# A graph network on one core: how often POOL waits for the landing of its own gathers and scatters

## The reference

```
h = maximum(layernorm(x), 0);  x = x + L0(h)   # three gcn hops and a product
h = maximum(layernorm(x), 0);  x = x + L1(h)   # mean over the edges, two layers with batch norm
h = maximum(layernorm(x), 0);  x = x + L2(h)   # six steps x = x + relu(agg/deg @ W.T + b)
h = maximum(layernorm(x), 0);  x = x + L3(h)   # two gcn hops with tanh between
```

## Time and profile before

| | us |
|---|---|
| median of 3 runs | 3292.27 (3290.51 to 3295.48) |
| the profiled execution | 3287.36 |
| its span | 3285.6 |
| POOL busy | 1442.2 (44%) |
| VectorE busy | 2032.4 (62%) |
| TensorE busy | 2527.2 (77%) |
| edge steps and hop 0, about | 19 to 749 |

### The profile page before, as it was taken

How to read it: one execution, slowest core, us unless ns; L and a number is a source line. 1 busy time by engine, 2 the same in 40 slices (tenths; PEclk the granted TensorE clock), 3 DMA queues, 4 the chain that set the end, 5 groups by cost and what they waited for, 6 DMA issues and landing times. The chain is left out here.

```text
span 3285.6 us, 46019 instructions
## 1 busy us (share of the span) xinstructions
PE 2527.2 (77%) x11251; PEld 1564.2 (48%) x11251; DVE 2032.4 (62%) x7784; ACT 1972.3 (60%) x4381; POOL 1442.2 (44%) x1507
## 2 busy tenths in 40 slices
PE   5767755558777678899999945799999999876840
PEld 2444434435555456445455422365655656543520
DVE  6544555558889766233333356687887878776630
ACT  1666755557777766455555558877777776764400
POOL 5555454545645264000000000176766767554576
PEclk8888877789888898899999966899999999987875
DMA  4655533445566565333333458866656656433311
GB/s 94 173 158 154 170 109 111 121 119 163 165 179 195 173 193 168 108 137 134 137 134 134 137 183 268 282 186 185 192 177 189 186 175 191 146 116 112 96 57 41
DMA packets 528965, 504.91 MB, mean 154 GB/s; under 512 B 58706, under 2 KB 389955, under 8 KB 528616
## 3 DMA queue, kind: packets, MB, share of 16 engines
q1 hardware_dynamic: 477388, 415.73, 39.2%
q0 software_dynamic: 47184, 85.73, 10.5%
q10 hardware_dynamic: 4172, 0.99, 0.2%
HBM read 246.45 MB, written 260.27 MB: 154 GB/s over the span
## 5 line engine op out<-in xcount | busy, mean ns | idle before, releaser
L1854 POOL DMA_INDIRECT h_G<-step_tab,row_i x294 | 287.1, 977 | 350.1 <-DMA step_tab<-l_NR 192.9
L1854 POOL DMA_INDIRECT h_M<-step_tab,row_i x294 | 284.3, 967 | 119.3 <-issue 86.3
L1567 DVE TENSOR_SCALAR b_Y<-b_BP,col 128x512 f32<-128x512 f32 x148 | 109.9, 742 | 354.5 <-PE b_BP L1521 354.5
L804 PE MATMUL a_PA<-a_H,w 128*128 128x512 f32 x504 | 263.2, 650 | 70.2 <-ACT a_H L968 63.4
L1549 ACT ACTIVATE b_Z<-b_BQ,bn 128x512 f32<-128x512 f32 x148 | 115.0, 777 | 256.7 <-PE b_BQ L1513 256.4
L1521 PE MATMUL b_BP<-b_Z,w 128*128 128x512 f32 x592 | 266.3, 592 | 0.0
L1609 POOL TENSOR_TENSOR b_d<-b_d,neghalf 128x1 f32<-128x1 f32 x1 | 0.6, 565 | 592.4 <-DVE b_d L1600 592.4
L2221 DVE TENSOR_TENSOR_SCAN h_T<-keep,h_T,h_P 128x512 f32<-128x512 bf16 x196 | 222.9, 1137 | 11.3 <-PE h_P L1972 2.1
L270 POOL DMA_INDIRECT h_G<-msg_tab,row_i x147 | 143.8, 978 | 195.5 <-issue 132.1
L239 ACT ACTIVATE a_NR<-a_XR,a_ln_nm,a_ln_rs 128x128 f32<-128x128 f32 x392 | 155.9, 485 | 106.3 <-DVE a_ln_nm L222 106.3
L239 ACT ACTIVATE a_HI<-a_X,a_ln_nm,a_ln_rs 128x128 f32<-128x128 f32 x490 | 201.0, 484 | 23.2 <-DVE a_ln_nm L222 23.2
(11 more groups left out here) (385 smaller groups left out, 6503.9 us busy)
## 6 DMA issues: line engine op xcount, KB each, us to landing
b_HI<-hin_tab SPq DMA_DIRECT2D x148, 256.0 KB, 2.8
y_tab<-b_Y SPq DMA_DIRECT2D x148, 256.0 KB, 2.0
l_Y<-y_tab SPq DMA_DIRECT2D x148, 256.0 KB, 4.0
l_X<-x_tab SPq DMA_DIRECT2D x148, 256.0 KB, 4.6
x_tab<-a_X SPq DMA_DIRECT2D x112, 256.0 KB, 4.3
hin_tab<-a_HI SPq DMA_DIRECT2D x112, 256.0 KB, 3.1
a_XR<-in_x SPq DMA_DIRECT2D x97, 256.0 KB, 4.5
out_rows<-l_O SPq DMA_DIRECT2D x97, 256.0 KB, 3.1
```

What stands on the lines that cost most here:

```text
L804: nc.tensor.matmul(PA[b][:, 0:nt * P], w[:, :], h[b][:, 0:nt, :].rearrange("p t d -> p (t d)"), start=True, stop=True).then_inc(done, 1)
L1567: nc.vector.tensor_scalar(Y[b][:, :], BP[b][:, :], col[:, C_B12:C_B12 + 1], None, ALU.add).then_inc(b_y, 1)
L1854: pool.indirect_dma_start(out=GR_[i % 2][b][:, k, :], out_offset=None, in_=table[:, :], in_offset=bass.IndirectOffsetOnAxis(ap=row_i[:, t ...
```

## The change

Four waits in POOL's program are dropped or thinned. In the E steps the wait for earlier scatters comes before every eighth scatter in place of every fourth. In `raw` the second half no longer waits until the first has landed. In hop 0 the last three slot reads no longer wait for the first four, and `raw(i + 1)` no longer waits for the slot reads. The waits for `x1`, for `sn.normed`, `xd_st`, `wd_set` and the one for `raw(i)` before the slot reads stay, and no transfer is added, dropped or moved.

```
                     for t in itertools.islice(scatters, NT if i == IT - 1 else 8):
-                        after(pool, slots_set, 16 * (t - t % 4))
+                        if t % 8 == 0:
+                            after(pool, slots_set, 16 * t)
                         pool.indirect_dma_start(out=node_tab[:, :], ...
...
                     after(pool, sn.normed, 2 * (i - 2) + b + 1)
                     after(pool, xd_st[i % 2][b], 16 * (i // 2))
-                    if b == 1:
-                        pool.wait_ge(xd_got[i % 2][0], 16 * SUB[0] * (i // 2 + 1))
                     for j in range(nt):
...
                 pool.wait_ge(xd_got[i % 2][1], 16 * SUB[1] * (i // 2 + 1))
                 for t in range(first_tile(i, 0), first_tile(i + 1, 0)):
-                    if t == first_tile(i, 1):
-                        pool.wait_ge(slot_got[i % 4], 16 * (sum(SUB) * (i // 4) + SUB[0]))
                     pool.indirect_dma_start(out=src_v[:, t, :], ...
-                pool.wait_ge(slot_got[i % 4], 16 * sum(SUB) * (i // 4 + 1))
                 if i + 1 < IT:
                     raw(i + 1)
```

## The result

The changed kernel takes 3177.33 us, the median of 4 runs (3170.21 to 3190.24), against 3291.4 for the kernel before (3290.51 to 3295.48, 4 runs): a ratio of 0.9654, 95% interval 0.9638 to 0.967. The forecast was 3185 with a range of 3173 to 3226. The profiled execution took 3173.83 us with a span of 3172.1, so its gain over the 3287.36 of before is 113.5 us, where the sum had 107.4. That holds for the chip it was timed on. On another, on which both kernels take longer, the changed one takes 1.0% more than the one before, which the last group of experiments is about.

A forecast was written before the change was run, and what follows sets the result against it. VectorE's 127.2 us of waits for POOL's gathers were taken as the bound up to 731 us. Edge steps and hop 0 steps of 20.9 us gave 107.4 us, so 3292.27 became 3185 us, range 3173 to 3226.

The forecast's parts named there:

- the sum: Whole kernel: edge-step and hop 0 savings put the last slot reads at 613.7 us instead of 721.06, a gain of 107.4 us.
- The edge steps: Before hop 0: 8.4 us from an earlier x1 and eight removed waits, 23.9 us, bring the first XD gather to 330.3 us.
- The landing of the last gathers in hop 0: POOL's wait before the slot reads in hop 0: taken as 3.76 us from the edge steps, between 2.2 and 5.2.
- the first rival: Edge steps and hop 0: landings grow with the burst, to 6.5 and 5.2 us; gain only 62.6 us, 3230 us; 14%.
- an estimate of 2.15 us: Landing of a 64 KB gather by the skill's rule; POOL's period falls under VectorE's 19.85 us, a gain of 115 us.
- The larger period rules, POOL's 20.9: Hop 0: POOL's period of 8.7 + 8.4 + 3.76 us sets the step, one microsecond over VectorE's.
- My second loop: Hop 0: VectorE's own step without its waits for XD, 19.85 us, with the 3.50 us wait for ScalarE's root kept.
- carried undiminished: After hop 0: later stages follow in a row with nothing of the change, so the 107.4 us gain reaches the end whole.
- a last third that takes a different time: Sign against the sum: the last third of the kernel takes a different time than before; no size given.
- the issues did not stretch: Rival on POOL's issues: packed against VectorE, a gather takes 1082 ns instead of 945; gain 67 us, 3225 us; 2%.
- the last rival: VectorE's chain shortens too: part of 74.6 us on products goes, with POOL's landing at its lower end; gain 125, 3167 us; 4%.
- The rival "slower": Hop 0: up to 15 transfers in flight delay each other; a landing of 11.5 us costs 27 us, 3319 us; 3%.

The follow-up runs named there:

- the last group of experiments: The unaltered changed kernel and three variants of it, on a chip where the kernel before takes 3620.19 us: unaltered 3664.94 us, variants 3739.19, 3680.78 and 3726.7 us.
- the runs meant to test it: Changed kernel with POOL held back once (3666.63 us), without landing waits (3755.2), with ScalarE's root earlier (3667.57), with both latter edits (3730.88); kernel before 3625.56 us there.

## Why the prediction was right

**The edge steps were 7.6 us better than worked out** (322.73 for 330.3). The gathers of step 5 start at 126.80, not 130.2, and were the ones bound by `x1`, as said (8.40 us of waiting). From there to the first `XD` gather it is 195.9 us, against 224.0 before, 28.1 less where the sum had 23.9. In the kernel before, POOL's waits of that stretch (138 to 363 us) are:

```profile
POOL node_tab L720 <- DMA a_XR<-in_x,src_i: 39.3, 9, 6.5
POOL node_tab L720 <- DMA node_tab<-own_v,end_i: 24.6, 8, 3.6
```

The eight removed waits were 24.6 us. The sum took them whole, though 0.3 us between two issues stays for each, so they give 22.2. The nine landing waits went from 39.3 to 33.9 us, 3.77 each, which gives another 5.4 that the sum did not have.

**The landing of the last gathers in hop 0 was the term mis-sized.** I took 3.76 us from the edge steps, between 2.2 and 5.2; it is 2.27. With it POOL's period is 8.7 + 8.4 + 2.3 = 19.4, and 19.47 is measured. The slot reads of step 13 start at 587.16 where the sum had 613.7; of these 26.5 us 7.6 come from the edge steps, 0.8 from the first landing and 13 x 1.39 = 18.1 from this. The prediction did name SP's traffic as what makes a landing long. Its mistake was to carry over the mean of the edge steps all the same, which mixes landings of 2.4 us, with SP quiet, and of 3.1 to 6.5, and not to ask where the last of seven gathers would fall: in the changed kernel that is behind SP's transfers. For the same reason the waits of four gathers were nearly twice those of three, which the first rival took as a sign of growth with the burst: those of three all stood where SP moved next to nothing (but for one at a share of 0.32). The rule of the Trainium skill in "DMA: Bandwidth & Descriptors", section "Anatomy of one DMA — SWDGE (gpsimd) path", from which the prediction had an estimate of 2.15 us, was nearer to hop 0 than my row was, and not to the edge steps, where 3.77 stayed.

**So VectorE rules, not POOL.** "The larger period rules, POOL's 20.9" did not come true. My second loop, 19.85 us, is measured at 19.75, and VectorE waits for no landing. POOL's is 0.3 shorter: its first slot read comes 15.0 us ahead of VectorE's root of the same step at step 1, and 17.9 ahead at step 13. The run with the hop's waits alone has the same two periods, 19.78 and 19.48. This rests on the profiles; the runs meant to test it did not. "What is late next is VectorE, with very little room" was right in kind. The second half of VectorE's statistics of step 13 starts at 597.6, forecast 605.7 by its own loop; 7.6 of the 8.1 us are again the edge steps.

**The gain is not carried undiminished.** VectorE's `s_ln_r` of step 13 is 122.8 us earlier than before (605.04 for 727.84). Two instructions of VectorE further on, in the kernel before:

```profile
1917.72 0.15 DVE L1590 TENSOR_SCALAR b_d<-b_d 128x1 f32<-128x1 f32 x1
...
3189.87 0.56 DVE L2268 TENSOR_TENSOR XS<-XS,l_PC 128x384 f32<-128x384 f32 x1 [0.44 <-PE l_PC L2006]
```

and after:

```profile
1797.17 0.15 DVE L1586 TENSOR_SCALAR b_d<-b_d 128x1 f32<-128x1 f32 x1
...
3076.66 0.55 DVE L2264 TENSOR_TENSOR XS<-XS,l_PC 128x384 f32<-128x384 f32 x1 [0.44 <-PE l_PC L2002]
```

The lead is 120.6 us at the end of the dense stage and 113.2 at the last rows. Compared instruction by instruction it goes in small steps: 2.7 us around the end of hop 0, 3.3 near 2100 us, and 6 between 2790 and 2970 after 2 were won. No instruction was changed there, and the runs of one kernel differ by 5 to 20 us, so two profiles can too; the cause stays open. The prediction named a last third that takes a different time as a sign that its sum is wrong, and by this profile it is, by some 7 us. For the profiled execution the sum had 3179.9 and 3173.83 was measured. These 6.1 us are the difference of the two: 15.4 us more won than summed in the first 600 us, 9.3 lost later. That the forecast came so close is in part luck, as the two errors cancel.

**The rivals.** The landing did not grow with the row, the issues did not stretch (944 ns on average for the 98 gathers of `XD`, for a median of 945 before), and the overlap of VectorE's chain was as in the last rival in its landing, but not in the 69.8 us on products. The rival "slower" had a mechanism of landings over 9.4 us. On the chip where the change is slower, the landings of hop 0 are 2.3 us as ever, and the instructions of the other engines come late. None of my cases had that, and a profile of one chip could not show it: there the idle time on "issue" is nothing.

## What to carry to other kernels

Waits for an engine's own transfers cost their landing each time, and the landing is a matter of what else moves at that moment: look at the windows around the issue before taking a figure from another stage, and do not take a mean over landings in and out of such traffic. Where several waits are dropped, work out the loop of the engine that consumes as well; here it was 0.3 us longer than the other, so that by the profile a shorter landing could not pay any more, which no run tested. Before a gain from back-to-back indirect transfers is taken for granted, time it on more than one chip, and look for idle time on "issue" in the engines that do not issue.

## What was not expected of the hardware

- The kernel before takes 3290 us where the change and its parts were timed, and 3620 and 3626 us on two other chips. In the dense stage, with POOL idle, the changed kernel runs alike to a matmul (464 in 150 us).
- On a chip of the slower kind TensorE passed one product in 2.8 us while POOL issued indirect transfers in an unbroken row of 46 us, with the DMA engines at a share of 0.15.
- Four gathers of `XD` landed in 4.0 us in one kernel and 4.9 in another that differs only in when they are issued; seven in a row landed in 2.27 and 2.61. In one kernel seven took 2.38 us with the queues at 14 GB/s and 6.52 with them at 320.
- The change is 3.5% faster on one kind of chip and 1.0% slower on the other.
